# Warm-up products put into TensorE's waits in a decoder of twelve sublayers

## The reference, cut to what matters

```python
x = x + L0_attn(layernorm(x))                  # rotary, causal, one head of 256
x = x + L0_xattn(ctx, ctx, layernorm(x))       # 16 heads of 16
x = x + L0_ffn(layernorm(x))                   # gates over 16 experts, causal attention of width 64
x = x + L1_attn(layernorm(x))                  # 16 heads of 16, causal
x = x + L1_xattn(layernorm(x), ctx, ctx)       # one head of 256
x = x + L1_ffn(layernorm(x))                   # ternary weights, gelu, layernorm over 1024
x = x + L2_attn(layernorm(x))                  # linear attention, cumulative sums
x = x + L2_xattn(layernorm(x), ctx, ctx)       # 16 heads of 64, masked
x = x + L2_ffn(layernorm(x))                   # router over 8 experts, the best one per token
x = x + L3_attn(layernorm(x))                  # 16 heads of 16, causal, rotary
x = x + L3_xattn(layernorm(x), ctx, ctx)       # one head of 256, masked keys
x = x + L3_ffn(layernorm(x))                   # four of 64 memory slots per token
```

## Time and profile before

| what | value |
|---|---|
| median of 3 runs | 4101.51 us (4095.73 to 4104.26) |
| the profiled execution | 4108.26 us, of it 4106.3 us from the first to the last instruction |
| TensorE, products busy | 3326.1 us, 81% of the span, 18369 instructions |
| TensorE, weight loads busy | 2148.7 us, 52% |
| VectorE busy | 2006.9 us, 49% |
| ScalarE busy | 1238.4 us, 30% |
| GpSimd busy | 427.5 us, 10% |
| mean granted clock of TensorE | 0.891 of full speed |
| warm-up products (L108) | 520, busy 192.0 us |

### The profile page before, as it was taken

The page is one execution under the profiler, slowest core; times in us unless marked ns, Lnnn a source line. Parts: engine busy times, 40 slices in busy tenths (PEclk is TensorE's granted clock), DMA queues, the critical chain, the costliest instruction groups (busy, mean ns, idle before and its releaser), DMA issues. The chain is left out here.

```text
span 4106.3 us, 48913 instructions
## 1 busy us (share of the span) xinstructions
PE 3326.1 (81%) x18369; PEld 2148.7 (52%) x18369; DVE 2006.9 (49%) x4645; ACT 1238.4 (30%) x2331; POOL 427.5 (10%) x413
## 2 busy tenths in 40 slices
PE   4878789678869967886996788699496888888888
PEld 2465555436555543655554365555395555454555
DVE  3664446466454646645554564555211535344343
ACT  1413226151322524132252413235131323222132
POOL 1010101111010111001010100101102001010100
PEclk9889899898989988898998889899698999898989
DMA  4000100200010020001002000100585020201101
GB/s 171 6 8 16 76 20 1 90 13 13 22 66 11 1 90 13 13 22 66 11 1 89 13 13 22 66 11 1 206 304 201 1 87 9 87 8 53 43 27 66
DMA packets 53212, 209.29 MB, mean 51 GB/s; under 512 B 4976, under 2 KB 37616, under 8 KB 41328
## 3 DMA queue, kind: packets, MB, share of 16 engines
q1 hardware_dynamic: 48128, 198.85, 13.0%
q0 software_dynamic: 1536, 4.20, 0.3%
q10 hardware_dynamic: 3312, 3.02, 0.2%
HBM read 186.89 MB, written 19.16 MB: 50 GB/s over the span
## 5 line engine op out<-in xcount | busy, mean ns | idle before, releaser
L785 DVE TENSOR_REDUCE nmax<-psum 128x1 f32<-128x512 f32 (+3 forms) x768 | 391.4, 551 | 157.4 <-PE psum L659 124.2
L307 POOL TENSOR_TENSOR rstd<-rstd,consts 128x1 f32<-128x1 f32 x160 | 88.2, 551 | 2204.6 <-DVE rstd L281 2204.6
L880 ACT ACTIVATE probs_odd<-psum 128x1024 f32<-128x1024 f32 x192 | 155.7, 811 | 271.7 <-PE psum L687 189.3
L108 PE MATMUL psum<-select 128*128 128x512 f32 x520 | 192.0, 502 | 49.8 <-PEq L120 49.8
L654 PE MATMUL psum<-ks,qs 64*128 64x512 f32 (+3 forms) x768 | 174.0, 447 | 61.8 <-DVE nmax L785 60.2
L329 ACT ACTIVATE xc<-psum 128x256 f32<-128x256 f32 x144 | 55.4, 385 | 543.6 <-PE psum L314 543.6
L1726 ACT ACTIVATE exps<-exps,nmax 128x512 f32<-128x512 f32 x256 | 183.3, 716 | 71.4 <-DVE nmax L1672 70.9
L1672 DVE CUSTOM_DVE_ANT_0 exps<-psum,mrows 128x512 f32<-128x512 f32 x256 | 166.1, 689 | 67.7 <-PE psum L1619 64.6
L880 ACT ACTIVATE probs_even<-psum 128x1024 f32<-128x1024 f32 x192 | 153.8, 811 | 111.2 <-PE psum L687 74.7
L654 PEld LDWEIGHTS psum<-ks,qs 64*128 64x128 f32 x768 | 75.1, 188 | 201.1 <-DVE nmax L785 120.8
L682 PE MATMUL psum<-qs,ks 64*128 64x512 f32 (+3 forms) x768 | 165.2, 422 | 6.8 <-ACT ks L846 5.9
(11 more groups left out here) (395 smaller groups left out, 6987.3 us busy)
## 6 DMA issues: line engine op xcount, KB each, us to landing
arena<-in_w SPq DMA_DIRECT2D x23, 1028.0 KB, 7.7
arena<-in_w SPq DMA_DIRECT2D x23, 1024.0 KB, 7.9
arena<-in_pack_L_ffn SPq DMA_DIRECT2D x4, 5184.5 KB, 15.0
arena<-in_pack_L_xattn SPq DMA_DIRECT2D x4, 4744.0 KB, 14.8
arena<-in_pack_L_ffn SPq DMA_DIRECT2D x4, 4120.0 KB, 12.3
arena<-in_pack_L_attn SPq DMA_DIRECT2D x5, 2432.0 KB, 9.0
arena<-in_pack_L_attn SPq DMA_DIRECT2D x9, 1280.0 KB, 5.7
arena<-ternary SPq DMA_DIRECT2D x4, 2056.0 KB, 7.7
```

The costliest lines, as they stand in the source:

```text
L108: pe.matmul(self.psum[:, bank, :], self.select[:, 0, :], self.select[:, 0:BANK // P, :], start=True, stop=True)
L785: dve.tensor_reduce(nmax[:, p, qt, n % 2:n % 2 + 1], net.psum[:, bank_of(s), 0:w], AX.X, ALU.max, negate=True).then_inc(row_read, 1)
L880: act.activation(probs(n)[:, :, lo:T], net.psum[:, first:first + 2, lo:T], ACT.Exp, scale=scale).then_inc(probs_done, 1)
```

## The change

`keep_warm` is called in more places, with the constants `WARM_STEP` = 3 (in place of `WARM_TAIL` = 2), `WARM_LAYERNORM` = 12 and `WARM_ROUTER` = 12:

- `turn_rest`: 3 products ahead of most tiles, 6 ahead of the tile that waits longest, and 3 behind the last tile, into a spare bank that `open_norm` is now told;
- `products`: 3 behind the last product, for a full table after a wait for the bank's earlier reader;
- `wide_attention` of width 64 (that is `L0_ffn`): 3 ahead of each `turn` but the first and 3 ahead of each `weigh`, 21 in all;
- `softmax_heads`: 2 ahead of each of the 8 column scores of the drain, and 3 ahead of the last `totals`, `spread_inverse` and `project` each;
- whole blocks of other engines get a list for TensorE: 12 where `L0_attn` rotates, 6 where `L1_ffn` copies its weights, 36 under its statistics, 24 under the mean squares and 24 under the routes of `L2_ffn`, 12 where `L3_xattn` makes its mask, 12 at the head of `change_batch`;
- the router of `L0_ffn`: 3 at its head, 12 behind the first product, and 36 in place of 24 behind the second.

The diff, without the changed calls of `open_norm` and the constants:

```diff
@@ products
                 mm.then_inc(product_done, 1)
+                if len(table) >= BANKS:
+                    last = len(table) - BANKS
+                    pe.wait_ge(act_done if owner[last] == "act" else dve_done, owner[:last + 1].count(owner[last]))
+                net.keep_warm(pe, WARM_STEP, bank=len(table) % BANKS)
@@ turn_rest
+    waits = {NT - 2: WARM_STEP, NT - 1: 2 * WARM_STEP} if first else {0: 2 * WARM_STEP}
     for t in range(first, NT):
-        norm.net.keep_warm(pe, WARM_TAIL, bank=norm.banks[NT - 1])
+        norm.net.keep_warm(pe, waits.get(t, WARM_STEP), bank=norm.banks[NT - 1])
         turn_tile(norm, pe, t)
+    norm.net.keep_warm(pe, WARM_STEP, bank=norm.spare)
@@ wide_attention
                 def turn(t):
+                    if t and width < D:
+                        net.keep_warm(pe, WARM_STEP, bank=score_banks[t - 1])
                     pe.wait_ge(probs_done, t + 1)
...
                 def weigh(t):
+                    if width < D:
+                        net.keep_warm(pe, WARM_STEP, bank=score_banks[t])
                     pe.wait_ge(copied_done, t + 1)
@@ softmax_heads
                         pe.wait_ge(stacked, outputs)
+                    if p >= PAIRS - lag:
+                        net.keep_warm(pe, 2, bank=3 + 2 * (n % 2))
                     lo = kt * P if causal else 0
...
                 weigh(GROUPS - 1, steps - 1)
+                net.keep_warm(pe, WARM_STEP, bank=3)
                 totals(GROUPS - 1)
+                net.keep_warm(pe, WARM_STEP, bank=3)
                 spread_inverse(GROUPS - 1)
+                net.keep_warm(pe, WARM_STEP, bank=3)
                 project(GROUPS - 1)
@@ L0_ffn, gates
             def _(pe):
+                net.keep_warm(pe, WARM_STEP)
                 pe.wait_ge(step, 1)
...
                 mm.then_inc(colsum_done, 1)
+                net.keep_warm(pe, WARM_ROUTER)
                 pe.wait_ge(sim_done, 1)
...
                 mm.then_inc(raw_done, 1)
-                net.keep_warm(pe, 2 * WARM_ROUTER)
+                net.keep_warm(pe, 3 * WARM_ROUTER)
@@ blocks in which TensorE had no work (one example)
+            @block.tensor
+            def _(pe):
+                net.keep_warm(pe, 3 * WARM_LAYERNORM)
@@ change_batch
                 def _(pe):
+                    net.keep_warm(pe, WARM_LAYERNORM)
                     pe.wait_ge(ctx_loaded, 16)
```

More of the change, by code:

```diff
@@ L40 @@
 BANKS = 8
-WARM_LAYERNORM, WARM_RECIPROCAL, WARM_ROUTER, WARM_TAIL = 12, 8, 12, 2
+WARM_LAYERNORM, WARM_RECIPROCAL, WARM_ROUTER, WARM_STEP = 12, 8, 12, 3
 PUT_AT = 6
@@ L251, in __init__, with open_norm @@
         self.net, self.x, self.xn, self.xc, self.need, self.parts, self.whole, self.room = net, x, xn, xc, need, parts, whole, room
-def open_norm(norm, sem, banks):
-    norm.banks = banks
+def open_norm(norm, sem, banks, spare):
+    norm.banks, norm.spare = banks, spare
     norm.stats_done, norm.mv_done, norm.guarded = sem("stats"), sem("mean and variance"), sem("variance + eps")
@@ L443, in wide_attention @@
             if norm is not None:
-                open_norm(norm, sem, score_banks)
+                open_norm(norm, sem, score_banks, 2)
                 @block.sync
@@ L600, in softmax_heads @@
             bias_done, added = sem("bias added to x"), sem("output of a tile added to x")
-            open_norm(norm, sem, (3, 4, 5, 6))
+            open_norm(norm, sem, (3, 4, 5, 6), 7)
             @block.sync
@@ L894, in divide_and_add @@
             scaled_done, out_done, added = sem("heads scaled"), sem("output product"), sem("output of a tile added to x")
-            open_norm(norm, sem, (0, 1, 2, 3))
+            open_norm(norm, sem, (0, 1, 2, 3), 4)
             @block.sync
@@ L955, in add_output @@
         out_done, added = sem("output of a tile"), sem("output of a tile added to x")
-        open_norm(norm, sem, (4, 5, 6, 7))
+        open_norm(norm, sem, (4, 5, 6, 7), 0)
         @block.sync
@@ L1317, in _ @@
                 fetch(start, sp)
+            @block.tensor
+            def _(pe):
+                net.keep_warm(pe, WARM_LAYERNORM // 2)
             @block.scalar
@@ L1829, in L2_ffn, with _ @@
             step, mean_done, root_done, rows_done = sem("step"), sem("mean square"), sem("1/root"), sem("rows")
+            @block.tensor
+            def _(pe):
+                net.keep_warm(pe, 2 * WARM_ROUTER)
             @block.sync
```

## The result

The changed kernel took 4165.02 us (median of 4 runs, 4155.33 to 4166.77), the kernel before 4099.32 us on the same chip: a ratio of 1.0155 (95% interval 1.0135 to 1.0174), about 66 us slower. 4074 us were forecast.

A forecast was written before the change was run, and what follows sets the result against it. TensorE, 81% busy at a mean clock of 0.891, was taken to bound the kernel. Costs of 84 us less gains of 112 us gave -28 us, from the 4101.5 us median to 4073.5 us; range 4043 to 4105 us.

The forecast's parts named there:

- product blocks' ends and the copy of the weights 0.5 in all: Cost per early batch of 3 products behind each table's last product, plus the weights' copy: 0.5 us.
- the attention of width 64: L0_ffn block: 21 products ahead of its steps cost 3.1 us a batch, starting at half clock and perhaps rising midway.
- L3_xattn's table: Product block of L3_xattn, 9.98 us long: full clock brings 7.6 us over four batches.
- the rivals: Costs hidden better, 0.14; gain and cost cancelling, 0.14; drains not holding, 0.10; other engines taking back the gain, 0.03.
- Drains and ends: Heads' column-score drains and final steps at full clock in all twelve blocks: drains near 25.4 us, costing 2.4, ends near 5.0.
- Starts: Sublayer blocks begin at full clock: L0_xattn's heads gain 6.6 us, L2_attn 4.6, L2_xattn's products 8.9, L0_attn's scores 6.5.
- Tables: L1_xattn's and L1_ffn's product blocks at full clock: near 11.3 and 8.5 us, gaining 6.7 and 10.7 over four batches.
- The bound that I left: Low bound for width 64: full clock from the start shortens the block, -0.9 us in all; half clock throughout gives +9.
- Gates: L0_ffn router block: 12 more products behind those that already end with VectorE, 2.9 us longer in full view.
- routes: L2_ffn block: 24 products outlast the other engines, +1.35 us, and 0.7 more for a thin gate block ahead: 2.05.
- The row phase: Long phase of the heads: clock counted as unchanged; a lower clock there was named as a sign of being wrong.
- The rule that speaks against it: Trainium skill: ramp penalty under 1% of a span, 41 us here; the sum would be +43 us and the change lose.

The follow-up runs named there:

- the kernel without the four lines: Changed kernel with the added wait and 3 warm-up products in `products` taken out: 4095.14 us, ratio 0.9988 to the kernel before.
- the tails alone: Kernel before plus only the new normalising tails (3 and 6 products ahead of tiles, 3 behind the last): 4079.89 us, ratio 0.9951.
- behind the loop: Changed kernel with the wait and 3 warm-up products in `products` once after the last product, not after every one: 4077.57 us, ratio 0.9946.
- The fastest kernel: Changed kernel with table products only after the last product, shorter lists (gates, L2_ffn, rotation, `change_batch`), no 21 products in width 64: 4054.74 us, ratio 0.9879.

## Why the prediction was wrong, and where it was right

The step that failed is one term of the cost, "product blocks' ends and the copy of the weights 0.5 in all". It was put on 3 products a table, behind its last product. The change runs 3 behind every product, 24 in a full table, in front of the next product, and makes PE wait for the first bank's reader: 6.77 us in L0_attn's table alone, at a clock of 1.00 in both kernels, where 0.5 us stood for all the tables of a batch and the copy together. Set right, the term is some 70 us against the kernel without the four lines (4165.02 - 4095.14) and 87 against the one that the prediction had in mind (4165.02 - 4077.57); it alone turns the sign. None of the rivals had it.

With the lines where the prediction took them to be, the kernel takes 4077.6 us; 4074 was worked out. That the two are so close is in part luck: by the trace the attention of width 64 cost 1 us in all where 12.4 were summed, while the 7.6 us of L3_xattn's table did not come and the heads' blocks got 14 us shorter where their starts, drains and ends were to bring 59.7 us at a cost of 28.8 in the drains. Step by step:

- *Drains and ends.* Right. All twelve drains are at 1.00, 25.0 us in L0_xattn, or 25.7 with the first two products (25.4 were forecast), and 23.5 in the causal ones; ends take 4.95 to 5.02. Three of the four drains of L0_xattn were at 1.00 in the kernel before too: the sum has a gain in one batch only and the cost, 2.4 us each, in all four.
- *Starts.* Right: 9.40, L2_attn 17.61, L2_xattn's products 42.49 (1.93 less, 2.2 forecast), L0_attn's scores 18.96. For L1_xattn's table, L2_attn and L2_xattn's products the tails are the source, by the run that has them alone and the one that lacks them. The starts of the heads are at 9.40 with the tails alone, but five of eight also without them. L0_attn's scores do not come from the tails: they take 20.23 us with the tails alone and 18.69 with the old ones behind the loop.
- *Tables.* L1_xattn 11.54 and L1_ffn 8.49 with the products behind the loop (11.3 and 8.5 forecast).
- *L3_xattn's table.* The gain comes, 9.89 to 8.22 us, and is lost at once: the next block waits for the mask. Behind the loop, in the timeline,

```profile
3274.54 0.34 SPq L2233 DMA_DIRECT2D raw<-in_key_mask  x1
3281.44 0.43 DVE L2240 TENSOR_SCALAR keep<-raw 128x512 f32<-128x512 uint8 x1 [6.12 <-DMA raw<-in_key_mask]
```

  the mask lands 6.9 us after its issue, where before it took 5.2 (3299.60 to 3304.78). The two blocks together take 16.4 us, as before 16.2. In both kernels the mask lands 15.3 us after the issue of the weights' load that starts with the table (3289.48 to 3304.78 before, 3266.18 to 3281.44 here), as if it waited for that load; no run isolates this. The 7.6 us of the forecast were not there; I had looked at what hid the twelve products beside the load, not at what the load hid.
- *Attention of width 64.* The bound that I left was nearer: 11.4 us, the -0.9 of a full clock from the start, in all four batches after the change; +3.0 in the one batch of the run behind the loop that starts low. The run without the 21 products shows that they were not worth their time at either start.
- *Gates* 1.5 to 2.7 us longer for 2.9, *routes* +1.2 for 2.05 (+1.8 behind the loop): sizes, not mechanism.
- *The row phase*, "which I count as unchanged", is not: in L1_attn it goes from 51.09 us at 1.00 to 54.68 at 0.94 in the batch shown, and takes back most of what start, drain and end gave there. Some 0.6 us of it are the drain's first two products, which this stretch holds (51.72 at 1.00 behind the loop); the rest goes with the clock. Where the fall lands differs between batches and kernels; what shifts it I have not isolated.
- *The rule that speaks against it.* The fastest kernel saves 46 us net, with all its warm-up products paid. The Trainium skill, "TensorE: Matmul & The Clock Gate", Part 1, "What's actually happening", puts the ramp penalty under 1% of a typical span, an estimate of 41 us here. The page says it of the products that run before the clock first rises; in this kernel the clock falls again in every batch, and 41 us were no bound here.

## What to carry to other kernels

Read a diff's added lines with their indentation before costing them: the same four lines are worth -18 us behind a loop and +70 in it. Put warm-up products where PE waits next to a change of block or for another engine, and judge each list by the length of its own block and of the next, not by the mean clock; a list that outlasts the other engines is paid in full. Look at what the next block waits for: a table that got faster gave nothing here, since the block behind it waits for a load.

## What the runs showed that I had not expected

One warm-up product in a run of its own costs 0.21 to 0.26 us at full clock; the same product alone among the products of 64 rows in the row phase costs 0.49 (5.92 us for twelve, at 1.00 in both). In the drain of L0_xattn, two at a time, sixteen cost 2.66 us, 0.17 each (27.01 against 24.35). And a block may stay at half clock from start to end though PE is busy for nearly all of it: 11.25 of 12.12 us in the attention of width 64, at 0.50.
